# Layer 2's recurrence in a decoder kernel: exponentials of ramps on ScalarE, products on VectorE, squares on ScalarE

## The chip, the cores and the metric

The kernel runs on one core of a Trainium2 chip. TensorE (PE in the rows) multiplies matrices, VectorE (DVE), ScalarE (ACT) and GpSimd (POOL) work elementwise, and each has its own queue; semaphores order them. The metric is the device time of one launch in microseconds (us), the median of three runs.

## What is computed

The program is a whole four-layer decoder on 8 sequences of 256 tokens with 128 channels. The change is in one stage of it, layer 2's time mixing and channel mixing:

```python
def step(carry, kv):                      # over the 256 tokens
    aa, bb, pp = carry
    kk, vv = kv
    ww = u + kk
    p = jnp.maximum(pp, ww)
    e1 = jnp.exp(pp - p)
    e2 = jnp.exp(ww - p)
    out = (e1 * aa + e2 * vv) / (e1 + e2 + EPS_WKV)
    p2 = jnp.maximum(pp, kk)
    e1b = jnp.exp(pp - p2)
    e2b = jnp.exp(kk - p2)
    aa_new = e1b * aa + e2b * vv
    pp_new = p2 + jnp.log(e1b + e2b + EPS_WKV)
    return ((aa_new, bb_new, pp_new), out)
...
x = x + r * wkv_out                       # r a sigmoid
h2 = layer_norm(x, ln2_g, ln2_b)
kc = time_shift(h2, cmix_k) @ Wk_c.T      # 128 -> 512
rc = jax.nn.sigmoid(time_shift(h2, cmix_r) @ Wr_c.T)
vv = jnp.square(jax.nn.relu(kc)) @ Wv_c.T
x = x + rc * vv
```

## The kernel before

`time_mixing` is written by hand: each engine's instructions stand in the order of its own function (`pe`, `dve`, `act`, `pool`), and nothing reorders them. An engine that waits holds up all that stands behind it in its queue.

Channels lie on the 128 partitions. The 2048 tokens are four parts of 512 columns, two sequences each; `FIRST` is parts 0 and 1, `LAST` is 2 and 3. A part has seven tiles of 512 columns (`kk`, `v`, `r`, `d`, `c`, `m`, `num`) in scratch and three padded ones in w_early: `pm` (running maximum), `sp` (running sum), `aa` (running weighted sum). The recurrence over tokens is a scan along the columns, two per part (one for each sequence), so four kinds of scan: maximum, sum, sum again with the small constant added, weighted sum.

Between the scans stand weights. With pp the level before a token, the weights are exp(pp - max(pp, k)) and exp(k - max(pp, k)), and a third pair with k + u. Before the change VectorE forms the maximum and one difference, GpSimd the other difference (`decay_pool`), ScalarE the two exponentials in place (`weights_act`), GpSimd the products (`value_pool`, `num_pool`), VectorE the sum, a reciprocal and the last two products (`gate_dve`). The logarithm of the sum is ScalarE's (`logs_act`).

Then TensorE turns `num` back (`num_pe`), VectorE adds it to XN and takes the statistics (`residual_dve`, `variance_dve`), ScalarE takes the square root, both scale, TensorE turns the halves (`turn_half_pe`), VectorE applies gain and bias (`affine_dve`). "second" is this normalisation for FIRST, "later" for LAST. The channel mixing runs in four quarters of 512 tokens: `up_pe` makes four groups of 512 columns (two banks in turn) and the receptance product, ScalarE's relu empties them into KC, GpSimd squares them, `down_pe` multiplies by the second matrix, VectorE multiplies by the receptance and adds to X. TensorE's order is up(0), down(0), num(2), up(1), num(3), down(1), turn of the later half, then up and down of quarters 2 and 3.

In the rows, an operation of a helper has the helper's line: L2501 is every scan, L469 every matmul, L318 the scaling on VectorE.

## Time and profile before

| | |
|---|---|
| time, median of 3 (lowest to highest) | 2234.5 us (2232.88 to 2235.41) |
| profiled execution: its time, its span | 2244.19 us, 2242.4 us |
| mean granted TensorE clock, as a share of full speed | 0.911 |
| stage: first scan to last down product | 1194.9 to 1336.5 us of the span |

The times of rows are those of the profiled execution. A stage in the middle of the program moves the end by as much as it gets shorter, since the next one waits for its last result.

### The profile page before, as it was taken

Reading aid. Unit: us, or ns where it says so; the run is one execution under the profiler, and the core shown is the slowest. Engines: PE = TensorE matmul, PEld = TensorE weight load, DVE = VectorE, ACT = ScalarE, POOL = GpSimd, SP = SyncE. Lnnn points to the kernel's source line nnn. Section 1 sums busy time; section 2 is a strip of 40 time slices with the busy share of each in tenths; the row PEclk is TensorE's granted clock in tenths of the full one; section 3 lists DMA queues with packets and bytes.
Section 4 is the critical chain, followed back from the end, with each engine's and each line's share of the span. In section 5 each row is a group of like instructions: output and inputs, shape, how many; then the busy total and the mean of one; then the engine's idle time right before and its main releaser. Section 6 shows DMA issues by size and latency. Waiting matters only on the chain.

```text
span 2242.4 us, 37692 instructions
## 1 busy us (share of the span) xinstructions
PE 1885.0 (84%) x13296; PEld 1250.2 (56%) x13296; DVE 1558.1 (69%) x3633; ACT 1285.2 (57%) x2737; POOL 652.3 (29%) x616
## 2 busy tenths in 40 slices
PE   7999775988999999949974288999997997589886
PEld 5777562446777777524452165566665676434465
DVE  5777685866777677458758947989997456478543
ACT  5777533776888878617755236677665212247622
POOL 3223003203544434342004532444343001221043
PEclk9999896998999999969987599999999898779898
DMA  4000004411000000035101000000000100354102
GB/s 196 1 1 2 1 1 129 138 37 38 1 1 1 1 1 1 1 90 155 58 1 77 0 1 1 1 2 1 1 1 22 36 1 1 120 164 114 57 24 78
DMA packets 80153, 87.37 MB, mean 39 GB/s; under 512 B 6578, under 2 KB 70115, under 8 KB 79073
## 3 DMA queue, kind: packets, MB, share of 16 engines
q1 hardware_dynamic: 78625, 82.49, 11.7%
q0 software_dynamic: 1344, 2.49, 0.4%
...
## 4 chain that ended last, share of the span: by engine, by line
PE 53%; DVE 29%; ACT 7%; issue 6%; POOL 2%; DMA 2%; SPq 0%; another core or an unknown queue 0%; DVEq 0%; ACTq 0%; POOLq 0%
PE bank L469 45%; DVE scratch L1221 5%; PE bank L653 2%; ACT XN L1996 2%; PE bank L2934 2%; PE bank L368 2%; DVE scratch L3052 1%; DVE scratch L3072 1%; PE bank L693 1%; DVE stats L245 1%; DVE XN L3092 1%; DVE scratch L1608 1%; DVE w_keep L1895 1%; ACT L2074 1%; DVE w_early L2501 1%
## 5 line engine op out<-in xcount | busy, mean ns | idle before, releaser
L469 PE MATMUL bank<-scratch 64*128 64x256 bf16 (+7 forms) x3056 | 340.2, 306 | 67.5 <-DMA scratch<-parts 39.4
L1221 DVE TENSOR_REDUCE scratch<-bank 128x2 f32<-128x512 f32 x384 | 244.6, 686 | 82.4 <-PE bank L469 79.8
L469 PEld LDWEIGHTS bank<-scratch 64*128 64x128 bf16 (+4 forms) x3056 | 184.1, 122 | 195.7 <-DVE scratch L1221 73.9
L469 PE MATMUL bank<-w_keep,scratch 128*128 128x128 f32 (+4 forms) x1760 | 245.4, 330 | 18.4 <-DVE scratch L1938 4.1
L1307 ACT ACTIVATE w_keep<-bank 128x512 f32<-128x512 f32 x384 | 212.6, 597 | 52.0 <-PE bank L469 44.3
L469 PE MATMUL bank<-XNT,w_keep 128*128 128x256 f32 (+4 forms) x800 | 238.0, 437 | 4.5 <-POOL w_keep L2135 2.2
L469 PEld LDWEIGHTS bank<-w_keep,scratch 128*128 128x128 f32 (+3 forms) x1760 | 182.7, 184 | 84.0 <-issue 55.6
L469 PEld LDWEIGHTS bank<-XNT,w_keep 128*128 128x128 f32 x800 | 149.9, 197 | 57.7 <-issue 28.4
L469 PE MATMUL bank<-w_early,scratch 64*128 64x256 f32 (+3 forms) x1152 | 164.8, 346 | 20.4 <-ACT w_early L3152 8.7
L469 PEld LDWEIGHTS bank<-w_early,scratch 64*128 64x128 f32 (+3 forms) x1152 | 120.0, 185 | 66.4 <-issue 25.6
L469 PE MATMUL bank<-w_keep 128*32 128x256 f32 (+1 forms) x1600 | 124.3, 386 | 11.3 <-ACT w_keep L1307 5.4
L469 PE MATMUL bank<-scratch,w_early 128*128 128x256 f32 (+2 forms) x416 | 124.7, 444 | 10.5 <-DVE scratch L2496 3.8
L795 ACT ACTIVATE scratch<-bank,scratch 128x256 f32<-128x256 f32 x256 | 100.3, 474 | 54.8 <-DVE scratch L721 54.8
L721 DVE TENSOR_REDUCE scratch<-bank 128x2 f32<-128x512 f32 x128 | 82.5, 686 | 61.8 <-PE bank L469 61.6
L3152 ACT ACTIVATE w_early<-bank,scratch 128x256 f32<-128x256 f32 x172 | 82.9, 562 | 72.1 <-DVE scratch L3056 72.1
L469 PE MATMUL bank<-XNT,w_early 128*128 128x256 f32 (+1 forms) x384 | 118.4, 439 | 4.5 <-ACT XNT L383 1.6
L3261 POOL TENSOR_TENSOR w_early<-w_early,scratch 128x1024 f32<-128x1024 f32 x43 | 81.4, 1893 | 137.2 <-DVE scratch L3077 137.2
L368 PE MATMUL bank<-w_keep,XN 128*128 128x128 f32 x192 | 48.8, 430 | 80.0 <-DVE XN L318 77.1
L3052 DVE TENSOR_REDUCE scratch<-bank 128x2 f32<-128x512 f32 x128 | 87.6, 684 | 22.9 <-PE bank L469 22.9
L469 PEld LDWEIGHTS bank<-scratch,w_early 128*128 128x128 f32 x416 | 72.5, 200 | 51.1 <-issue 30.6
L735 POOL TENSOR_TENSOR scratch<-scratch 128x1024 f32<-128x1024 f32 x32 | 61.5, 1952 | 127.3 <-DVE scratch L751 127.3
L469 PEld LDWEIGHTS bank<-XNT,w_early 128*128 128x128 f32 x384 | 73.1, 201 | 44.7 <-issue 30.5
...
## 6 DMA issues: line engine op xcount, KB each, us to landing
...
```

The lines of the kernel that those rows point to most:

```text
L368: t = pe.transpose(k.bank[q][:, j * P:(j + 1) * P], src(i), k.w["ident"])
L469: return pe.matmul(out, lhsT, rhs, start=start, stop=stop, skip_group_check=True)
L653: m = pe.transpose(self.k.bank[3 + o][:, c * S + t * P:c * S + (t + 1) * P], self.expo[g % 4][:, t * S + c * P:t * S + (c + 1) * P], self. ...
L721: dve.tensor_reduce(self.neg[g % 4], self.scores(g)[:, :].rearrange("p (t s) -> p t s", s=S), AXX, ALU.max, negate=True).then_inc(*s.maxed ...
L735: return pool.tensor_tensor(self.kron[n][t].rearrange("p (h i j) -> p h i j", i=HD, j=HD), a, c, ALU.mult)
L795: a = act.activation(self.expo[g % 4][:, t * S:(t + 1) * S], self.scores(g)[:, t * S:(t + 1) * S], ACT.Exp, bias=self.neg[g % 4][:, t:t + 1])
L1221: dve.tensor_reduce(neg[:, :, h], self.k.bank[5 - g % 2][:, :].rearrange("p (t s) -> p t s", s=S), AXX, ALU.max, negate=True).then_inc(*s. ...
L1307: act.activation(self.expo[g % 8], k.bank[g % 4][:, :], ACT.Exp, scale=HD ** -0.5).then_inc(*s.weighed.up("e", g))
L1996: a = act.activation(self.by_head(self.early[u % 2])[:, t, h, :], self.upto, ACT.Copy, scale=a3[:, t, h:h + 1])
L3052: dve.tensor_reduce(neg, self.k.bank[o][:, :].rearrange("p (t s) -> p t s", s=S), AXX, ALU.max, negate=True).then_inc(*s.maxed.up("x", p, o))
L3152: a = act.activation(self.weights(p, o)[:, t * S:(t + 1) * S], self.k.bank[o][:, t * S:(t + 1) * S], ACT.Exp, bias=self.bias[p % 2][:, o * ...
L3261: pool.tensor_tensor(ex, ex, self.sums[p % 2].unsqueeze(2).to_broadcast([P, 2 * HALVES, S]), ALU.mult).then_inc(*s.pool.up("scaled", p))
```

## The change

The weights are written without a maximum. With x = k - pp, exp(pp - max(pp, k)) is exp(-relu(x)) and exp(k - max(pp, k)) is exp(-relu(-x)); the third pair has k + u in the place of k, which is a bias of u and of -u. So VectorE makes one difference x per part (`ahead_dve`), and ScalarE two relus and two exponentials for each pair (`ramps_act`). The level is not written back: the logarithm of the sum before the token is subtracted from x (`level_dve`). All products go from GpSimd to VectorE. The reciprocal becomes Ln and Exp with scale -1 on ScalarE (`inverse_act`); the square root and reciprocal of "second" and "later" become Ln and Exp with scale -0.5 (`log_root_act`). One table set with Ln and Exp is loaded ahead of the inputs and again after the sigmoids of `r`. The squares of the channel mixing go from GpSimd to ScalarE, each behind the next group's relu (`relu_act`, `square_act`), and the receptance sigmoids of quarters 0 and 1 behind all relus of the two. GpSimd keeps the folding of weights, with one more column (`minus_u`), and the four residual adds, each now as soon as the part's XN is there. The queues of VectorE, ScalarE and TensorE are written anew:

```diff
-    def first_decay_dve(dve, part):
-        (_, _, _, d, _, _, _), (pm, _, _) = streams[part]
+    def ahead_dve(dve, part):
+        (kk, v, r, d, c, x, num), (pm, sp, aa) = streams[part]
+        k3 = b3(kk)
+        dve.wait_ge(*s.stacked.at("in", part, 0))
+        scan(dve, part, pm, k3, k3, BEFORE_ALL, ALU.max, ALU.max).then_inc(*s.vector.up("p", part))
         dve.wait_ge(*s.vector.at("p", part))
-        dve.tensor_tensor(b3(d), pm[:, :, 0:S], pm[:, :, 1:PADDED], ALU.subtract).then_inc(*s.formed.up("d", part))
+        dve.tensor_tensor(b3(x), k3, pm[:, :, 0:S], ALU.subtract).then_inc(*s.formed.up("x", part))
...
+        dve.wait_ge(*s.vector.at("s", part))
+        dve.tensor_tensor(b3(num), b3(d), sp[:, :, 0:S], ALU.mult).then_inc(*s.vector.up("ds", part))
...
+    def level_dve(dve, part):
+        (kk, v, r, d, c, x, num), _ = streams[part]
+        dve.wait_ge(*s.scalar.at("log", part))
+        dve.tensor_tensor(x, x, num, ALU.subtract).then_inc(*s.formed.up("x2", part))
+
+    def weigh_dve(dve, part):
+        (kk, v, r, d, c, x, num), (pm, sp, aa) = streams[part]
+        dve.wait_ge(*s.weighed.at("second", part))
+        dve.wait_ge(*s.stacked.at("in", part, 1))
+        dve.tensor_tensor(c, c, v, ALU.mult).then_inc(*s.vector.up("cv", part))
+        dve.wait_ge(*s.vector.at("cv", part))
+        scan(dve, part, aa, b3(d), b3(c), 0.0, ALU.mult, ALU.add).then_inc(*s.vector.up("a", part))
+
+    def whole_dve(dve, part):
+        (kk, v, r, d, c, x, num), _ = streams[part]
+        dve.wait_ge(*s.weighed.at("third", part))
+        dve.scalar_tensor_tensor(out=x, in0=num, scalar=1e-8, in1=kk, op0=ALU.add, op1=ALU.add).then_inc(*s.vector.up("den", part))
+
+    def gate_dve(dve, part):
+        (kk, v, r, d, c, x, num), (pm, sp, aa) = streams[part]
+        dve.wait_ge(*s.vector.at("a", part))
+        dve.wait_ge(*s.vector.at("den", part))
+        dve.tensor_tensor(b3(num), b3(num), aa[:, :, 0:S], ALU.mult).then_inc(*s.vector.up("da", part))
+        dve.tensor_tensor(v, v, kk, ALU.mult).then_inc(*s.vector.up("vc", part))
+        dve.wait_ge(*s.vector.at("vc", part))
+        dve.wait_ge(*s.vector.at("da", part))
+        dve.tensor_tensor(num, num, v, ALU.add).then_inc(*s.vector.up("num", part))
+        dve.wait_ge(*s.scalar.at("inverse", part))
+        dve.wait_ge(*s.vector.at("num", part))
+        dve.tensor_tensor(num, num, x, ALU.mult).then_inc(*s.vector.up("out", part))
...
-        inverse_dve(k, dve, tag)
+        dve.wait_ge(*s.deviation.at(tag))
...
-        pe.wait_ge(*s.pool.at("squared", 4 * q + 3))
+        pe.wait_ge(*s.scalar.at("squared", 4 * q + 3))
...
+            ahead_dve(e, part)
+        for part in FIRST:
             sums_dve(e, part)
-        raised_dve(e, FIRST)
-        level_dve(e, FIRST)
-        raised_dve(e, LAST)
-        weigh_dve(e, FIRST)
-        level_dve(e, LAST)
-        gate_dve(e, FIRST)
-        weigh_dve(e, LAST)
+            raised_dve(e, part)
+        level_dve(e, 0)
+        sums_dve(e, 2)
+        level_dve(e, 1)
+        raised_dve(e, 2)
+        weigh_dve(e, 0)
+        sums_dve(e, 3)
+        whole_dve(e, 0)
+        weigh_dve(e, 1)
+        whole_dve(e, 1)
+        raised_dve(e, 3)
+        gate_dve(e, 0)
+        gate_dve(e, 1)
+        for part in LAST:
+            level_dve(e, part)
         residual_dve(e, "second", FIRST)
         scale_dve(k, e, "second", k.XN, O2, range(0, NT // 2))
+        weigh_dve(e, 2)
         affine_dve(e, "second", "r_g2", "r_b2", FIRST)
-        gate_dve(e, LAST)
+        weigh_dve(e, 3)
+        for part in LAST:
+            whole_dve(e, part)
+        for part in LAST:
+            gate_dve(e, part)
         residual_dve(e, "later", LAST)
...
+    def ramps_act(act, tag, part, x, down, up, first_bias, second_bias):
+
+        act.activation(down, x, ACT.Relu, bias=first_bias).then_inc(*s.lowered.up(tag, "down", part))
+        act.activation(up, x, ACT.Relu, bias=second_bias, scale=-1.0).then_inc(*s.lowered.up(tag, "up", part))
+        act.wait_ge(*s.lowered.at(tag, "down", part))
+        act.activation(down, down, ACT.Exp, scale=-1.0)
+        act.wait_ge(*s.lowered.at(tag, "up", part))
+        act.activation(up, up, ACT.Exp, scale=-1.0).then_inc(*s.weighed.up(tag, part))
+
+    def weights_act(act, tag, part):
+        (kk, v, r, d, c, x, num), _ = streams[part]
+        act.wait_ge(*s.formed.at("x" if tag == "first" else "x2", part))
+        if tag == "second":
+            act.wait_ge(*s.vector.at("s2", part))
+        if tag == "third":
+            ramps_act(act, tag, part, x, num, kk, w["r_u"], minus_u)
+        else:
+            ramps_act(act, tag, part, x, d, c, 0.0, 0.0)
+
+    def inverse_act(act, part):
+        (_, _, _, _, _, x, _), _ = streams[part]
+        act.wait_ge(*s.vector.at("den", part))
+        act.activation(x, x, ACT.Ln).then_inc(*s.lowered.up("den", part))
+        act.wait_ge(*s.lowered.at("den", part))
+        act.activation(x, x, ACT.Exp, scale=-1.0).then_inc(*s.scalar.up("inverse", part))
+
+    def log_act(act, part):
+        (_, _, _, _, _, _, num), (_, sp, _) = streams[part]
+        act.wait_ge(*s.vector.at("s2", part))
+        act.activation(b3(num), sp[:, :, 0:S], ACT.Ln).then_inc(*s.scalar.up("log", part))
+
+    def log_root_act(act, tag):
+        act.wait_ge(*s.variance.at(tag))
+        act.activation(k.rs[:, :], k.moments[:, 2, :], ACT.Ln, bias=k.small[:, 0:1], scale=1.0 / P).then_inc(*s.lowered.up("root", tag))
+        act.wait_ge(*s.lowered.at("root", tag))
+        act.activation(k.rs[:, :], k.rs[:, :], ACT.Exp, scale=-0.5).then_inc(*s.deviation.up(tag))
...
+        weights_act(e, "first", 0)
+        input_act(e, 3, 0)
+        weights_act(e, "first", 1)
+        input_act(e, 0, 1)
+        weights_act(e, "first", 2)
+        input_act(e, 1, 1)
+        weights_act(e, "first", 3)
+        input_act(e, 2, 1)
+        input_act(e, 3, 1)
...
+        log_act(e, 0)
+        log_act(e, 1)
+        weights_act(e, "second", 0)
+        weights_act(e, "second", 1)
+        weights_act(e, "third", 0)
+        weights_act(e, "third", 1)
+        log_act(e, 2)
+        inverse_act(e, 0)
+        inverse_act(e, 1)
...
+        e.preload_act_table_set("natural_log_exp_and_others")
+        log_act(e, 3)
+        weights_act(e, "second", 2)
+        weights_act(e, "second", 3)
+        log_root_act(e, "second")
+        scale_act(k, e, "second", k.XN, O2, range(0, NT // 2))
+        weights_act(e, "third", 2)
+        weights_act(e, "third", 3)
+        relu_act(e, 0)
+        relu_act(e, 1)
+        inverse_act(e, 2)
+        relu_act(e, 2)
+        inverse_act(e, 3)
+        for u in (3, 4, 5):
+            relu_act(e, u)
+        log_root_act(e, "later")
+        scale_act(k, e, "later", k.XN, O2, range(NT // 2, NT))
+        for u in (6, 7):
+            relu_act(e, u)
+        for q in range(QUARTERS):
+            if q >= 2:
+                for u in range(4 * q, 4 * q + 4):
+                    relu_act(e, u)
+            receptance_act(e, q)
...
+    def relu_act(act, u):
+        q, g = divmod(u, 4)
+        act.wait_ge(*s.projected.at("kc", u))
+        if q >= 2 and g == 0:
+            act.wait_ge(*s.multiplied.at("vv", q - 2))
+        act.activation(KC[q % 2][:, g * BANK:(g + 1) * BANK], k.bank[u % 2][:, :], ACT.Relu).then_inc(*s.gated.up("relu", u))
+        if g:
+            square_act(act, u - 1)
+        if g == 3:
+            square_act(act, u)
+
+    def square_act(act, u):
+        q, g = divmod(u, 4)
+        kg = KC[q % 2][:, g * BANK:(g + 1) * BANK]
+        act.wait_ge(*s.gated.at("relu", u))
+        act.activation(kg, kg, ACT.Square).then_inc(*s.scalar.up("squared", u))
...
-            for g in range(4):
-                u, kg = 4 * q + g, KC[q % 2][:, g * BANK:(g + 1) * BANK]
-                e.wait_ge(*s.gated.at("relu", u))
-                e.tensor_tensor(kg, kg, kg, ALU.mult).then_inc(*s.pool.up("squared", u))
+            e.wait_ge(*s.added.at("num", q))
```

VectorE, where parts 0 and 1 are divided and gated. Before (L2549 sum, L2551 reciprocal, L2554 and L2557 products, L2501 the weighted scan of part 2):

```order
L2549 SCALAR_TENSOR_TENSOR scratch<-scratch 128x512
L2551 RECIPROCAL scratch<-scratch 128x512
L2554 TENSOR_TENSOR scratch<-scratch 128x512
L2557 TENSOR_TENSOR scratch<-scratch 128x512
L2549 SCALAR_TENSOR_TENSOR scratch<-scratch 128x512
L2551 RECIPROCAL scratch<-scratch 128x512
L2554 TENSOR_TENSOR scratch<-scratch 128x512
L2557 TENSOR_TENSOR scratch<-scratch 128x512
L2501 SCALAR_TENSOR_TENSOR w_early<-scratch 128x256 x2
```

and now (L2552 and L2553 the two products, L2556 their sum, L2559 times the inverse, L2562 times `r`, L2533 the level of parts 2 and 3):

```order
L2552 TENSOR_TENSOR scratch<-scratch,w_early 128x512
L2553 TENSOR_TENSOR scratch<-scratch 128x512
L2556 TENSOR_TENSOR scratch<-scratch 128x512
L2559 TENSOR_TENSOR scratch<-scratch 128x512
L2562 TENSOR_TENSOR scratch<-scratch 128x512
L2552 TENSOR_TENSOR scratch<-scratch,w_early 128x512
L2553 TENSOR_TENSOR scratch<-scratch 128x512
L2556 TENSOR_TENSOR scratch<-scratch 128x512
L2559 TENSOR_TENSOR scratch<-scratch 128x512
L2562 TENSOR_TENSOR scratch<-scratch 128x512
L2533 TENSOR_TENSOR scratch<-scratch 128x512 x2
```

The reciprocals have gone from VectorE's queue, GpSimd's three products and sums of each part have come into it, and the weighted scans of parts 2 and 3 stand further back.

ScalarE, where the logarithms and the second weights of parts 0 and 1 stand. Before (L2741 Ln, L2748 and L2749 exponentials, L2751 the added u):

```order
L2741 ACT_TABLE_LOAD
L2741 ACTIVATE scratch<-w_early 128x512 x2
L2748 ACT_TABLE_LOAD
L2748 ACTIVATE scratch<-scratch 128x512
L2749 ACTIVATE scratch<-scratch 128x512
L2751 ACTIVATE scratch<-scratch,w_keep 128x512
L2748 ACTIVATE scratch<-scratch 128x512
L2749 ACTIVATE scratch<-scratch 128x512
L2751 ACTIVATE scratch<-scratch,w_keep 128x512
L2741 ACT_TABLE_LOAD
```

and now (L2710 copies of v, L2741 Ln, L2714 and L2715 relus, L2717 and L2719 exponentials):

```order
L2710 ACTIVATE scratch<-bank 128x512 x2
L2741 ACTIVATE scratch<-w_early 128x512 x2
L2714 ACTIVATE scratch<-scratch 128x512
L2715 ACTIVATE scratch<-scratch 128x512
L2717 ACTIVATE scratch<-scratch 128x512
L2719 ACTIVATE scratch<-scratch 128x512
L2714 ACTIVATE scratch<-scratch 128x512
L2715 ACTIVATE scratch<-scratch 128x512
L2717 ACTIVATE scratch<-scratch 128x512
```

Three table loads have gone here, and each pair of exponentials has two relus ahead of it.

ScalarE, at the first quarter of the channel mixing. Before (L2759 relu, L2763 sigmoid):

```order
L284 ACTIVATE small<-small 128x1
L2759 ACTIVATE scratch<-bank 128x512 x4
L2763 ACTIVATE scratch<-bank 128x512
L2759 ACTIVATE scratch<-bank 128x512 x4
L2763 ACTIVATE scratch<-bank 128x512
```

and now (L2809 relu, L2819 square, L2734 Ln and L2736 Exp of the inverse of parts 2 and 3):

```order
L2809 ACTIVATE scratch<-bank 128x512 x2
L2819 ACTIVATE scratch<-scratch 128x512
L2734 ACTIVATE scratch<-scratch 128x512
L2736 ACTIVATE scratch<-scratch 128x512
L2809 ACTIVATE scratch<-bank 128x512
L2819 ACTIVATE scratch<-scratch 128x512
L2734 ACTIVATE scratch<-scratch 128x512
L2736 ACTIVATE scratch<-scratch 128x512
L2809 ACTIVATE scratch<-bank 128x512
L2819 ACTIVATE scratch<-scratch 128x512 x2
```

The squares and two inverses now stand between the relus; the sigmoids have moved behind quarter 1.

TensorE, from the end of down(0) to the end of down(1), as a difference (L2613 and L2618 are `num_pe`, L2620 and L2625 `turn_half_pe`; the 512-wide matmuls are up(1), the x16 row is down(1)):

```order
-L2613 MATMUL bank<-w_keep,scratch 128x128 x4
+L2618 MATMUL bank<-w_keep,scratch 128x128 x8
 L469 MATMUL bank<-scratch,w_early 128x512 x8
 L469 MATMUL bank<-w_early,scratch 128x128 x8
-L2613 MATMUL bank<-w_keep,scratch 128x128 x4
+L2625 MATMUL bank<-w_keep,scratch 128x128 x8
 L469 MATMUL bank<-w_keep,scratch 128x128 x16
-L2620 MATMUL bank<-w_keep,scratch 128x128 x8
```

num(3) has moved ahead of up(1), and the later half's transposes ahead of down(1).

## Rows read from the trace of the kernel before

**Rows 1.** The page, busy time, share and instructions by engine.

```profile
PE 1885.0 (84%) x13296; PEld 1250.2 (56%) x13296; DVE 1558.1 (69%) x3633; ACT 1285.2 (57%) x2737; POOL 652.3 (29%) x616
```

**Rows 2.** Windows: length, PE PEld DVE ACT POOL busy (count), clock, DMA, GB/s.

```profile
1194.00:1208.50 14.50, 14.50 (x33) 6.33 (x32) 11.49 (x14) 7.50 (x13) 5.90 (x5) 0.92 0.00 1
1208.50:1268.80 60.30, 7.95 (x22) 3.68 (x20) 59.21 (x58) 24.08 (x37) 32.89 (x22) 0.57 0.00 0
1268.80:1280.40 11.60, 2.06 (x8) 1.50 (x8) 10.70 (x26) 5.69 (x10) 8.40 (x7) 0.50 0.00 0
1280.40:1286.00 5.60, 5.54 (x8) 2.48 (x9) 5.43 (x5) 0.60 (x1) 1.05 (x1) 0.58 0.00 0
1286.00:1337.00 51.00, 49.43 (x266) 34.14 (x264) 22.48 (x48) 17.37 (x29) 21.02 (x20) 1.00 0.00 1
```

**Rows 3.** Groups by line, VectorE, 1208.5 to 1268.8: busy, mean ns, idle before.

```profile
L2501 DVE TENSOR_TENSOR_SCAN w_early<-scratch 128x256 f32<-128x256 f32 x22 | 19.4, 933 | 0.4 <-ACT scratch L2705 0.2
L2551 DVE RECIPROCAL scratch<-scratch 128x512 f32<-128x512 f32 x2 | 6.7, 3353 | 0.1
```

**Rows 4.** One line of VectorE: min/median/max ns, first and last start.

```profile
L2531 DVE TENSOR_TENSOR scratch<-w_early,scratch x4: 692/1079/1632, 1221.6 to 1246.6; 128x512 f32<-128x512 f32 x4
```

**Rows 5.** Timeline of VectorE: start us, us, line, operation, idle before.

```profile
1207.04 1.28 DVE L2501 TENSOR_TENSOR_SCAN w_early<-scratch 128x256 f32<-128x256 f32 x2 [0.39 <-ACT scratch L2705]
...
1218.32 0.67 DVE L2518 TENSOR_TENSOR scratch<-scratch 128x512 f32<-128x512 f32 x1
1219.01 0.69 DVE L2520 SCALAR_TENSOR_TENSOR scratch<-scratch 128x512 f32<-128x512 f32 x1
1219.74 1.27 DVE L2501 TENSOR_TENSOR_SCAN w_early<-scratch 128x256 f32<-128x256 f32 x2
1220.93 0.67 DVE L2529 TENSOR_TENSOR w_early<-w_early,scratch 128x512 f32<-128x512 f32 x1
...
1222.97 1.67 DVE L2529 TENSOR_TENSOR w_early<-w_early,scratch 128x512 f32<-128x512 f32 x1
...
1268.83 0.68 DVE L2566 TENSOR_TENSOR XN<-XN,bank 128x512 f32<-128x512 f32 x1
...
1272.37 1.24 DVE L256 TENSOR_TENSOR moments<-moments 128x16 f32<-128x16 f32 x1
...
1276.09 2.38 DVE L318 TENSOR_SCALAR scratch<-XN,rs,moments 128x128 f32<-128x128 f32 x5
1278.74 1.66 DVE L2496 TENSOR_SCALAR scratch<-bank,w_keep 128x512 f32<-128x512 f32 x2 [0.27 <-PE bank L2620]
```

**Rows 6.** Timeline of GpSimd.

```profile
1222.40 1.68 POOL L2771 TENSOR_TENSOR scratch<-w_early,scratch 128x512 f32<-128x512 f32 x1 [5.86 <-DVE scratch L2531]
```

**Rows 7.** Timeline of ScalarE.

```profile
1198.80 0.60 ACT L2698 ACTIVATE scratch<-bank 128x512 f32<-128x512 f32 x1 [1.12 <-PE bank L469]
...
1204.57 1.28 ACT L2704 ACT_TABLE_LOAD   x1
1205.86 0.63 ACT L2704 ACTIVATE scratch<-scratch 128x512 f32<-128x512 f32 x1
1206.40 0.61 ACT L2705 ACTIVATE scratch<-scratch 128x512 f32<-128x512 f32 x1
...
1225.48 0.71 ACT L2751 ACTIVATE scratch<-scratch,w_keep 128x512 f32<-128x512 f32 x1
...
1274.87 0.31 ACT L278 ACTIVATE rs<-moments,small 128x16 f32<-128x16 f32 x1 [2.22 <-DVE moments L258]
```

**Rows 8.** One line of ScalarE, Square of 128x512 in another stage.

```profile
L2031 ACT ACTIVATE w_keep<-scratch x32: 612/613/663, 555.2 to 930.6; 128x512 f32<-128x512 f32 x32
```

**Rows 9.** Timeline of TensorE: up(0), up(2), down(3).

```profile
1280.46 9.42 PE L469 MATMUL bank<-scratch,w_early 128*128 128x512 f32 x16 [0.90 <-DVE scratch L2496]
...
1311.24 7.13 PE L469 MATMUL bank<-scratch,w_early 128*128 128x512 f32 x16 [1.00 <-DVE scratch L2496]
...
1332.69 3.84 PE L469 MATMUL bank<-w_keep,scratch 128*128 128x128 f32 x32
```

156 lines of the change are left out of this document (20 added, 136 removed).

## The prediction

> **What bounds the kernel now.** I began with the busy shares [rows 1]: TensorE has most of the span, so a change that touches VectorE, ScalarE and GpSimd can only pay where TensorE waits for them. The table of windows over this stage shows where that is [rows 2]. From 1208.5 to 1268.8 TensorE is busy 7.95 of 60.3 us and VectorE 59.21: the recurrence runs at VectorE's pace. From 1286 to 1337 it is the reverse (TensorE 49.43 of 51.0 us). So two places count: the instant at which the channel mixing starts on TensorE, now 1280.46 [rows 9], and the length of its tail, which ends at 1332.69 + 3.84 = 1336.5 [rows 9], 56.1 us later.
>
> Next I asked why VectorE needs 60 us. The window has 58 instructions [rows 2]. A pair of scans alone takes 1.27 us and a two-input instruction of 512 columns 0.67 [rows 5]; 22 scans, two reciprocals (6.7 us [rows 3]) and 34 others make 14.0 + 6.7 + 22.8 = 43.5 us. VectorE was busy 59.2, so 15.7 us are excess; the scans alone show 19.4 for 14.0 [rows 3], and line 2531 lies between 692 and 1632 ns for one shape [rows 4]. The pattern is in the timeline: line 2529 at 1220.93 takes 0.67; the same line at 1222.97 takes 1.67 [rows 5], and a GpSimd tensor_tensor ran from 1222.40 to 1224.08 [rows 6]. 1224.08 plus 0.58 is 1224.66, when the slow one ended. VectorE stood still until GpSimd was done.
>
> **A rule beside it.** The Trainium skill, SBUF — State Buffer, section "SBUF: two separate sides", says the same as a rule: the port pair is an exclusive lock for a whole instruction, between GpSimd and a VectorE instruction with two SBUF inputs. By that rule the excess goes with GpSimd's work; were it instead the cost of these access patterns, the sum would be that of the second rival below.
>
> **The change, step by step.** Steps between instructions, from the four consecutive rows 1218.32 to 1220.93 [rows 5]: 0.70 us where the next waits for the result (0.73 for scalar_tensor_tensor), 1.19 for a scan pair, so 0.60 for each instruction whose successor doesn't wait. On ScalarE an activation of 512 columns starts 0.54 after the one before [rows 7]; I use 0.52, the step when the later one needs 0.61, and allow 0.15 more for a Ln whose Exp waits.
>
> *A, the head.* Before, the first weights wait for a table load at 1204.57 [rows 7] and the sums start at 1207.04 [rows 5]. After, the table is loaded in ScalarE's idle time before the first copy. The third copy is at 1198.80 [rows 7]; the four activations of part 0 follow (2.1 us, to 1201.4), then the copy of part 3, to 1202.0. VectorE then does that part's two scans and its subtraction (1.27 + 0.04 + 0.58) and starts the sums at 1203.9. Part 0's weights were ready 2 us earlier. Gain 3.2 us.
>
> *B, VectorE's queue from the sums to the first residual.* Before it is 1207.04 to 1268.83 [rows 5], 61.8 us. After, by the order, it has 50 instructions: 7 for each of four parts (sums and raised), 4 subtractions (level), 3 for each of parts 0 and 1 (weigh), 2 (whole), 10 (gate). 22 have a successor that waits, 4 of them scalar_tensor_tensor: 18 x 0.70 + 4 x 0.73 + 28 x 0.60 = 32.3 us. No GpSimd instruction runs here, so no excess. Gain 29.5 us. Check by what goes away: 15.7 excess, 6.9 of reciprocals (two, 3.35 and a gap each), and 58 other instructions become 50, which is the remaining 7. The divisions go to ScalarE as Ln and Exp. Does it keep pace? Per part and tag a ramp costs 4 x 0.52 = 2.1 us. Following both queues, part 0's second weights are ready at 1215.9 and wanted at 1218.9, part 1's third at 1222.4 and wanted at 1225, and the receptance copies, with a 1.28 us load [rows 7] on either side, end about 1230 and are wanted at 1231. ScalarE has 2 to 3 us in hand, 1 us at the last; so its 12 ramps (25 us) and the two loads cost nothing. Without that cover each us would count.
>
> *C, normalisation.* Before, 11.6 us [rows 2]. The two small instructions held up at 1272.37 (1.24 us and the next like it) [rows 5], against 0.17 free, give back 2.1; the scale, 2.38 with GpSimd at work [rows 5], gives back 1.0 (estimate: five steps of 0.27). Square root and reciprocal become Ln and Exp of 128x16: 0.31 by the nearest row [rows 7], about 0.1 more than before. The weigh of part 2 now stands between scale and affine: 0.70 + 1.19 = 1.9, of which 0.5 covers the wait for the transposes that the affine had at 1278.74 [rows 5]. GpSimd's residual add of part 1 now runs while the variance starts: +0.3. Sum 10.2, gain 1.4. New waits here are ScalarE's: behind its wait for the variance stand the third ramps of parts 2 and 3 and the first relu; ScalarE is free 3.4 us ahead of the mixing's start, the relu's input comes 3.8 us after it, and the two ramps need 4.2 of those 7.2 us.
>
> *D, the tail.* TensorE's matmuls are the same. One wait goes: the 1.00 us before 1311.24 [rows 9], since the later half's transposes now stand ahead of the second down product, which covers VectorE's affine. One comes: down(0) waits for the last square. On ScalarE, after relu 1 come squares, relus and two Ln-Exp pairs, ten more activations, about 12.1 us after the start; TensorE arrives at 11.2. Cost 0.95. In later quarters only two squares follow the last relu: 0.60 + 2 x 0.52 + 0.1 = 1.75 us against the 1.8 us of receptance matmuls, like GpSimd's square now. A Square from SBUF is 613 ns at another line [rows 8]. The transposes num(2) and num(3) find VectorE finished 3 us earlier. Relus 6 and 7 stand behind ScalarE's wait for the later variance: root and scale end 26 us after the start, as relu 7's input comes. The receptance sigmoids of quarters 0 and 1 now stand behind those relus and a table load; what they hold up, two products of VectorE, isn't wanted by TensorE until quarter 2's receptance matmuls, 10 us later. Net 0.
>
> Sum 3.2 + 29.5 + 1.4 + 0 = 34.1 us. The profiled execution took 2244.2 us (span 2242.4), 9.7 above the median of 2234.5; a sum of rows from it should read 2210 there and 2200.4 as a median.
>
> **Bounds.** ScalarE's ramps may cost 0.71 a step, the price of its one activation with a per-partition bias, without overlap [rows 7]: then the first ramps, the root, and the ten activations before down(0) all lengthen, 3.8 us in all: 2204.2. TensorE's clock is 0.50 before the mixing, 0.58 until 1286 and 1.00 after [rows 2]. If it rises at once at the start, the first 5.3 us of matmuls shrink by half (−2.6); if 3 us later, +1.5. If down(0) doesn't wait, −0.95. So 2197 to 2205.5 as the likeliest case's own range.
>
> **Rivals.**
> *ScalarE becomes the bound* (8%): 40 us of activations stand in 51 us. At 0.6 us a step it still hides; at 1.0 each wait for weights opens and the gain falls to 15: 2219. For it: three times as many exponentials and relus. Against: the rows of 0.61 to 0.63.
> *The excess isn't GpSimd's* (4%): if shape or address makes 15.7 us, they stay: 2216. Against: the same line at 0.67 and 1.67.
> *The clock doesn't come up* (2%), the one that ends slower. Place: the mixing's start, after idle time with only eight transposes in it. Tail matmuls busy 49.4 us at 1.00 [rows 2] would need up to 49 us more at 0.50: 2234.5 − 34 + 49 = 2249. It decides from 34 us of work at the low clock. Against: the same sequence of transposes, scale, transposes, affine rose within 5.5 us now. The Trainium skill, TensorE: Matmul & The Clock Gate, section "What's actually happening", states that throttled is the default and activity releases it; this trace agrees, 0.50 then 1.00.
> *More goes than I count* (8%): the clock comes early and part 3's work is better hidden: 2195 to 2197.
> The likeliest has 78%. About 0.2% (4.5 us) is what a measurement can tell here: faster 96%, same 2%, slower 2%. Range 2195.5 to 2205.5.
>
> **What would show it.** Right: between the sums and the first residual VectorE has no instruction of 512 columns over 0.75 us, and about 32 us pass; the mixing starts near 1246; ScalarE never ends a VectorE wait over 1 us before that; one gap of about 1 us ahead of down(0), none ahead of up(2). Wrong: activations steps over 0.6 us, long scans with GpSimd idle, a table load between relus, or a PEclk under 1.00 more than 8 us into the mixing.

## The result, and the profile after

The changed kernel takes 2193.26 us, the median of 4 runs (2191.42 to 2196.38), against 2234.78 us for the kernel before (4 runs): a ratio of 0.9817, 95% interval 0.98 to 0.9834. The sign and the mechanism were as forecast; the gain, 41.5 us, is larger than the 34.1 us of the sum, and the time lies below the range. The profiled execution took 2194.88 us where 2210 was forecast for it.

The windows over the stage, cut where its phases change, answer to [rows 2]:

```profile
1195.30:1208.50 13.20, 13.20 (x32) 5.85 (x31) 12.13 (x19) 10.30 (x21) 0.00 (x0) 0.98 0.01 2
1208.50:1236.50 28.00, 7.86 (x22) 3.71 (x20) 27.24 (x44) 20.25 (x35) 0.00 (x0) 0.64 0.00 0
1236.50:1246.20 9.70, 2.17 (x9) 1.49 (x8) 8.87 (x28) 9.13 (x20) 2.54 (x2) 0.50 0.00 0
1246.20:1249.70 3.50, 3.50 (x4) 1.51 (x5) 3.46 (x6) 1.04 (x3) 0.00 (x0) 0.50 0.00 0
1249.70:1300.80 51.10, 50.22 (x269) 34.88 (x267) 19.75 (x51) 26.40 (x48) 2.54 (x2) 0.99 0.00 1
```

VectorE is still what sets the pace up to the mixing (27.24 of 28.0 us busy), but the stretch is less than half as long (28.0 us for 60.3). GpSimd is silent in it. The mixing is TensorE's, as before.

VectorE's timeline answers to [rows 5]: the start of the sums, the first residual, the variance, scale and affine, and the only wait over 1 us before the gating of part 3 is done (1259.2).

```profile
1203.92 1.27 DVE L2503 TENSOR_TENSOR_SCAN w_early<-scratch 128x256 f32<-128x256 f32 x2
...
1236.57 0.68 DVE L2571 TENSOR_TENSOR XN<-XN,bank 128x512 f32<-128x512 f32 x1
...
1239.68 0.44 DVE L252 TENSOR_TENSOR moments<-stats 128x16 f32<-128x16 f32 x1
...
1241.45 1.37 DVE L318 TENSOR_SCALAR scratch<-XN,rs,moments 128x128 f32<-128x128 f32 x5
...
1244.64 1.50 DVE L2498 TENSOR_SCALAR scratch<-bank,w_keep 128x512 f32<-128x512 f32 x2
...
1254.38 0.69 DVE L2559 TENSOR_TENSOR scratch<-scratch 128x512 f32<-128x512 f32 x1 [3.21 <-ACT scratch L2736]
```

From 1203.92 to 1236.57 are 32.65 us, forecast 32.3. The one long wait, 3.21 us for L2736 (the inverse of part 2), begins after the mixing has started, and TensorE wants that part only at 1261.79.

The groups of VectorE in that stretch answer to [rows 3] and [rows 4]; the columns are busy us, mean ns:

```profile
L2503 DVE TENSOR_TENSOR_SCAN w_early<-scratch 128x256 f32<-128x256 f32 x20 | 12.5, 675 | 0.2
L2533 DVE TENSOR_TENSOR scratch<-scratch 128x512 f32<-128x512 f32 x4 | 2.6, 680 | 0.0
```

ScalarE's timeline answers to [rows 7]: first weights, a ramp with a per-partition bias, the two table loads around the receptance copies, and the square root's place.

```profile
1188.52 1.28 ACT L2756 ACT_TABLE_LOAD   x1
...
1199.31 0.62 ACT L2714 ACTIVATE scratch<-scratch 128x512 f32<-128x512 f32 x1
1199.83 0.62 ACT L2715 ACTIVATE scratch<-scratch 128x512 f32<-128x512 f32 x1
...
1218.55 0.70 ACT L2714 ACTIVATE scratch<-scratch,w_keep 128x512 f32<-128x512 f32 x1
...
1226.62 0.63 ACT L2736 ACTIVATE scratch<-scratch 128x512 f32<-128x512 f32 x1
1227.27 1.28 ACT L2710 ACT_TABLE_LOAD   x1
1228.57 2.06 ACT L2710 ACTIVATE scratch<-bank 128x512 f32<-128x512 f32 x4
1230.65 1.28 ACT L2779 ACT_TABLE_LOAD   x1
...
1240.65 0.31 ACT L2745 ACTIVATE rs<-moments,small 128x16 f32<-128x16 f32 x1 [0.30 <-DVE moments L258]
```

A step is 0.52 us (1199.31 to 1199.83), or 0.61 with the bias of u (1218.55 to 1219.16). TensorE's timeline answers to [rows 9]:

```profile
1246.20 9.25 PE L469 MATMUL bank<-scratch,w_early 128*128 128x512 f32 x16 [2.30 <-DVE scratch L2498]
...
1258.11 3.84 PE L469 MATMUL bank<-w_keep,scratch 128*128 128x128 f32 x32 [0.87 <-ACT scratch L2819]
...
1271.32 1.04 PE L2625 MATMUL bank<-w_keep,scratch 128*128 128x128 f32 x8
1272.19 3.74 PE L469 MATMUL bank<-w_keep,scratch 128*128 128x128 f32 x32
1275.76 7.03 PE L469 MATMUL bank<-scratch,w_early 128*128 128x512 f32 x16
...
1296.95 3.28 PE L469 MATMUL bank<-w_keep,scratch 128*128 128x128 f32 x27
```

The mixing starts at 1246.20 (forecast: near 1246), there is one gap, 0.87 us ahead of down(0), and none ahead of up(2) at 1275.76.

**The ledger of the stage.** Measured in each trace from GpSimd's first instruction of the stage (1180.94 before, 1180.49 after), so that what lies ahead of it drops out:

| phase | before | after | gain | forecast |
|---|---|---|---|---|
| A, to the first sum | 26.10 | 23.43 | 2.67 | 3.2 |
| B, to the first residual | 61.79 | 32.65 | 29.14 | 29.5 |
| C, to the mixing | 11.63 | 9.63 | 2.00 | 1.4 |
| D, to the end of down(3) | 56.07 | 54.59 | 1.48 | 0 |
| stage | 155.59 | 120.30 | 35.29 | 34.1 |

The spans of the two profiled executions differ by 49.3 us (2242.4 and 2193.1). 0.45 lie ahead of the stage, 35.3 in it, and 13.6 behind it, where no instruction was changed. Two places hold nearly all of the 13.6. The first is the next stage. Its first TensorE work, of before:

```profile
1344.20 1.96 PE L368 MATMUL bank<-w_keep,XN 128*128 128x128 f32 x8 [7.67 <-DVE XN L318]
...
1349.60 3.75 PE L469 MATMUL bank<-w_keep,scratch 128*128 128x512 f32 x4 [1.19 <-DVE scratch L3046]
```

and after:

```profile
1308.07 1.96 PE L368 MATMUL bank<-w_keep,XN 128*128 128x128 f32 x8 [7.28 <-DVE XN L318]
...
1313.47 1.95 PE L469 MATMUL bank<-w_keep,scratch 128*128 128x512 f32 x4 [1.30 <-DVE scratch L3065]
```

The four matmuls at 1349.60 took 3.75 us, the same ones at 1313.47 take 1.95. That is 1.8 of a 2.2 us difference; the other 0.4 lie in the idle time ahead of the first transposes (7.67 and 7.28). The second is the program's last stage. A window that ends 35 us before the end, of before and then after:

```profile
2177.40:2207.40 30.00, 24.62 (x119) 18.22 (x120) 7.71 (x24) 9.65 (x19) 14.85 (x16) 0.77 0.11 30
```

```profile
2128.10:2158.10 30.00, 28.38 (x172) 22.52 (x173) 9.08 (x27) 12.65 (x24) 22.90 (x23) 1.00 0.17 48
```

Before had 119 matmuls there at a clock of 0.77, after has 172 at 1.00. TensorE's rows around the start of that window, of before:

```profile
2175.85 0.33 PE L3665 MATMUL bank<-w_keep 128*128 128x128 f32 x1
...
2177.79 1.16 PE L469 MATMUL bank<-w_keep,w_early 128*128 128x320 f32 x3 [1.15 <-issue]
2179.95 1.46 PE L469 MATMUL bank<-w_keep,w_early 128*128 128x320 f32 x2 [1.00 <-issue]
...
2193.13 0.49 PE L3665 MATMUL bank<-w_keep 128*128 128x128 f32 x3
```

and of the second profile of the same kernel (the first run of the next section):

```profile
2175.73 0.44 PE L3665 MATMUL bank<-w_keep 128*128 128x128 f32 x2
...
2181.16 0.49 PE L3665 MATMUL bank<-w_keep 128*128 128x128 f32 x3
```

The same work takes 17.3 us in the first profile of before and 5.4 in its second (5.4 in the changed kernel too): a loss of 11.9 us. Behind this place the changed kernel takes 0.7 more, so 11.2 of the 13.6 lie in the last stage.

### The profile page after: what moved, and what is told of

It is laid out like the page before. It is cut to its first block, busy times and chain, and to the rows that moved or that the text cites. A ratio compares the mean times of both kernels' runs of the same rounds, so it can differ in the third digit from the quotient of the medians.

```text
span 2193.1 us, 37675 instructions
## 1 busy us (share of the span) xinstructions
PE 1875.5 (86%) x13296; PEld 1246.2 (57%) x13296; DVE 1522.1 (69%) x3631; ACT 1299.4 (59%) x2773; POOL 588.4 (27%) x569
## 4 chain that ended last, share of the span: by engine, by line
PE 54%; DVE 28%; ACT 7%; issue 5%; POOL 3%; DMA 2%; SPq 0%; DVEq 0%; POOLq 0%; ACTq 0%
PE bank L469 45%; DVE scratch L1221 5%; PE bank L653 2%; ACT XN L1996 2%; DVE scratch L3071 2%; PE bank L368 2%; DVE scratch L3091 2%; PE bank L2953 2%; PE bank L693 1%; DVE stats L245 1%; DVE XN L3111 1%; DVE scratch L1608 1%; DVE w_keep L1895 1%; ACT L2074 1%; PE bank L1190 1%
## 5 line engine op out<-in xcount | busy, mean ns | idle before, releaser
L469 PE MATMUL bank<-w_keep 128*32 128x256 f32 (+1 forms) x1600 | 124.2, 386 | 11.2 <-ACT w_keep L1307 5.4
L1895 DVE SCALAR_TENSOR_TENSOR w_keep<-w_keep,w_early 128x256 f32<-128x256 f32 x192 | 97.2, 556 | 0.1
```

Of the source, the lines that this page charges most:

```text
L469: return pe.matmul(out, lhsT, rhs, start=start, stop=stop, skip_group_check=True)
L1895: o = dve.scalar_tensor_tensor(out=yv[:, j, :], in0=xv[:, j, tap:tap + S], scalar=scale, in1=yv[:, j, :], op0=ALU.mult, op1=ALU.add)
```

## The experiments

Each kernel was compared with runs of the kernel before on the same chip; three chips were used, on which the kernel before read 2231.9 us (17 runs; the two repeats, products, squares), 2229.83 us (7 runs; reciprocal, order, inverses, folding) and 2244.08 us (9 runs; the last four). So a time is read through its ratio, and through the length of the stage in its trace. The changed kernel as it is ran on the first of the three only, so the edited ones of the other two are set against it by ratio and by stage.

### The two kernels again

The kernel before, unchanged.

> The kernel before, unchanged, for a second profile. The change gained 41.5 us, of which its own stage shows 35.3 and 6 us lie in later stages that it doesn't touch. Theory (the surplus is not the change's: TensorE's clock and one stall in the last stage fell unluckily in the profile shown): the ratio is 1.00 within 0.2%, this profile's stage again takes 155.6 us from its first instruction to the last down product, and the 11 us that the first profile lost between 2178 and 2204 us are mostly gone. Rival (the change does something for the later stages): the loss of 11 us between 2178 and 2204 is there again.

Measured: 2233.76 us (10 runs), ratio 1.0011, interval 0.9997 to 1.0025; stage 155.69 us. Its profiled execution has a span of 2230.6 where the first one had 2242.4, and the same window of the last stage reads

```profile
2165.60:2195.60 30.00, 28.22 (x170) 22.11 (x169) 9.25 (x27) 13.13 (x25) 23.00 (x24) 1.00 0.17 48
```

with 170 matmuls at 1.00. The loss of 11.9 us is not the kernel's. Nor is it one execution's alone: on the third chip the kernel before reads 2244, and the four profiles taken there (the last four runs) all show such a loss, with 119 to 125 matmuls at a clock of 0.77 to 0.83 in this window.

The changed kernel, unchanged.

> The changed kernel, unchanged, for a second profile. Theory: ratio 0.981 to 0.985; the stage takes 120.3 us again within 0.3; what differs from the first profile differs in the later stages, where the low stretches of TensorE's clock lie elsewhere. Rival: all of it repeats to 0.5 us, later stages too, so that the 6 us are a fixed property of the program.

Measured: 2193.93 us (2189.6 to 2196.8), ratio 0.984, interval 0.9812 to 0.9868; stage 120.17 us. On this chip the gain in medians is 2231.9 - 2193.9 = 38.0 us. The two repeated profiles differ by 35.5 us in the stage and by 2.5 behind it (894.1 and 891.6 us from the last down product to the end), and the four matmuls of the next stage again take 3.75 and 1.95. So what lies behind the stage repeated nearly as the rival had it (892.3 and 891.6 in the two profiles of the changed kernel), but only 2.5 of the expectation's 6 us are there.

### Who held VectorE up

The kernel before, with the products and differences of the recurrence moved from GpSimd to VectorE; reciprocals, maxima and exponentials stay. For each part:

```diff
+        dve.wait_ge(*s.vector.at("s", part))
+        dve.tensor_tensor(b3(m), b3(d), sp[:, :, 0:S], ALU.mult).then_inc(*s.vector.up("ds", part))
...
+            dve.tensor_tensor(b3(d), P0, b3(m), ALU.subtract)
...
+            dve.tensor_tensor(c, c, v, ALU.mult).then_inc(*s.vector.up("cv", part))
...
+            dve.tensor_tensor(b3(num), b3(d), aa[:, :, 0:S], ALU.mult).then_inc(*s.vector.up("da", part))
+            dve.tensor_tensor(v, v, c, ALU.mult).then_inc(*s.vector.up("vc", part))
+            dve.tensor_tensor(num, num, v, ALU.add).then_inc(*s.vector.up("num", part))
...
-        decay_pool(e, "second", FIRST)
-        value_pool(e, FIRST)
-        decay_pool(e, "third", FIRST)
-        num_pool(e, FIRST)
...
```

> The kernel before with only GpSimd's elementwise work of the recurrence moved to VectorE, in its place in the order (maxima, differences, reciprocals and GpSimd's squares stay). Theory (VectorE stood still for GpSimd): between the sums and the first residual VectorE gets 22 instructions more (+14.3 us) and loses the excess of 15.7 us, no 512-column instruction except the reciprocals over 0.75 us; the normalisation loses 3 us more: 4 to 6 us faster, ratio 0.997 to 0.998. Rival (the long instructions are long by shape or address): they stay long, 14 us slower, ratio 1.006.

Measured: 2222.67 us, ratio 0.9962, interval 0.9944 to 0.9979; stage 148.97 us, 6.6 shorter (3.0 between the sums and the first residual, 3.6 in the normalisation), somewhat more than the 4 to 6 expected. VectorE's groups from the sums to the first residual, and the window:

```profile
L2501 DVE TENSOR_TENSOR_SCAN w_early<-scratch 128x256 f32<-128x256 f32 x24 | 15.3, 678 | 2.0 <-ACT scratch L2716 1.7
L2564 DVE RECIPROCAL scratch<-scratch 128x512 f32<-128x512 f32 x2 | 6.7, 3352 | 0.1
L2533 DVE TENSOR_TENSOR scratch<-w_early,scratch 128x512 f32<-128x512 f32 x4 | 2.8, 692 | 0.1
L2531 DVE TENSOR_TENSOR w_early<-w_early,scratch 128x512 f32<-128x512 f32 x4 | 2.7, 680 | 0.0
1207.00:1266.30 59.30, 9.95 (x26) 4.48 (x25) 57.53 (x83) 26.19 (x40) 0.00 (x0) 0.59 0.00 0
```

L2531 and L2533 here are the lines 2529 and 2531 of before. The second of them took 692 to 1632 ns for one shape [rows 4] and takes 692 on average now; scans have gone from 933 [rows 3] to 678. From the first sum (1207.54 here) to the first residual (1266.29) VectorE has 82 instructions where it had 60, and needs 58.75 us where it needed 61.79. The 22 added ones cost about 14 us (estimate: 0.60 to 0.70 each), so about 17 of excess went with GpSimd's work, for the 15.7 of the sum. The excess was GpSimd's; that shapes or addresses make it is refuted. The Trainium skill, SBUF — State Buffer, section "SBUF: two separate sides", describes this as a lock that whoever starts first holds for the whole instruction. The traces agree: L2529 took 1.67 us at 1222.97 beside a GpSimd instruction of 1.68 [rows 5] [rows 6], and takes 0.68 on average here, with GpSimd silent.

The same numbers give the worth of the rest, by subtraction and not by a run of its own: from this kernel's 58.75 us to the changed kernel's 32.65 are 26.1 us, of which the reciprocals are 6.4 (next run) and about 20 are the 30 instructions that the ramps and the new differences make needless.

### The divisions on VectorE

The changed kernel, with the reciprocals back on VectorE and the inverses gone from ScalarE.

```diff
-        dve.wait_ge(*s.scalar.at("inverse", part))
-        dve.wait_ge(*s.vector.at("num", part))
+        dve.reciprocal(x, x).then_inc(*s.vector.up("inverse", part))
+        dve.wait_ge(*s.vector.at("inverse", part))
```

> The changed kernel with the divisions back as reciprocals on VectorE (3.35 us each), no Ln and Exp for them. Theory (the sum's term of 6.9 us for two reciprocals is right, those of parts 2 and 3 lie beside TensorE's up(0) and down(0)): the first residual comes 6.9 us later; in the tail the gap ahead of down(0) goes (-0.9) and num(3) may come up to 1.2 us late; stage 127 us against 120.3. Rival (the Ln and Exp pairs only moved the time to ScalarE): stage below 123.

Measured: 2202.15 us, ratio 0.9882, interval 0.9853 to 0.9911; stage 127.16 us, 6.9 longer: 6.4 before the first residual, 0.4 in the tail, where the gap ahead of down(0) is gone and one of 0.89 us stands ahead of num(3). ScalarE is freer by two pairs of activations before that residual and gives nothing for it. So the inverses on ScalarE are hidden, and the part of B that the prediction put to the reciprocals, 6.9, measures 6.4.

### The squares on GpSimd

The changed kernel, with the squares where they were: `square_act` isn't called, GpSimd waits for each relu and multiplies, `down_pe` waits for GpSimd. GpSimd's residual adds stand behind the squares again.

```diff
-        if g:
-            square_act(act, u - 1)
-        if g == 3:
-            square_act(act, u)
...
+            for g in range(4):
+                u, kg = 4 * q + g, KC[q % 2][:, g * BANK:(g + 1) * BANK]
+                e.wait_ge(*s.gated.at("relu", u))
+                e.tensor_tensor(kg, kg, kg, ALU.mult).then_inc(*s.pool.up("squared", u))
```

> The changed kernel with the squares of the channel mixing back on GpSimd. Theory: the gap ahead of down(0) shrinks from 0.9 us to near 0, since a GpSimd square ends 1.7 us after the last relu's input and TensorE has 1.8 us of receptance matmuls; VectorE's gating of parts 2 and 3 gets 1 us instructions here and there under cover. Against the changed kernel 0 to 1 us faster: ratio 0.981 to 0.983. Rival (the squares on ScalarE bring part of the gain): ratio over 0.985.

Measured: 2198.8 us (2192.44 to 2199.34), ratio 0.9853, interval 0.9825 to 0.9881; stage 119.97 us, 0.3 shorter. down(0):

```profile
1247.39 9.44 PE L469 MATMUL bank<-scratch,w_early 128*128 128x512 f32 x16 [2.30 <-DVE scratch L2498]
1256.67 1.95 PE L469 MATMUL bank<-w_early,scratch 128*128 128x128 f32 x16
1258.97 3.28 PE L469 MATMUL bank<-w_keep,scratch 128*128 128x128 f32 x27 [0.35 <-POOL scratch L2838]
```

It waits 0.35 us instead of 0.87. In the stage, moving the squares brought nothing and costs 0.3 us, but that isn't all down(0)'s: 0.26 of it lie in the normalisation, where the residual add no longer stands in the way of L252 (0.19 us here, 0.44 in the changed kernel), and in quarters 2 and 3 the squares on ScalarE save 0.16. The ratio came out on the rival's side (over 0.985), and the median 4.9 us above the changed kernel's on the same chip; the intervals overlap, and the profiles differ by 2.8 us ahead of the stage and 3.8 behind it, where the two programs are the same. So the runs can't tell the two kernels apart.

### TensorE's order of before

The changed kernel, with num(3) behind up(1) and the later half's transposes behind down(1) again; ScalarE's relus 6 and 7 stand ahead of its later scale, as they must then.

```diff
         num_pe(e, 2)
+        up_pe(e, 1)
         num_pe(e, 3)
-        up_pe(e, 1)
+        down_pe(e, 1)
         turn_half_pe(e, "later", (2, 3))
-        down_pe(e, 1)
...
```

> The changed kernel with TensorE's order of before: num(3) behind up(1), the later half's transposes behind down(1), and ScalarE's relus 6 and 7 ahead of its wait for the later variance. Theory (the tail's 1.5 us come from the order: a wait of 1.0 us ahead of up(2) gone, and transposes that take 0.87 us of TensorE where I had counted 1.57): the wait of 1.0 us is back, the tail from up(0) to the last down product is 56 us against 54.6, the stage 121.7 us. Rival (the order does nothing, the tail got shorter elsewhere): 54.6 again.

Measured: 2199.75 us, ratio 0.9858, interval 0.9826 to 0.9891; stage 122.58 us, 2.3 longer, nearly all of it in the tail (56.8 against 54.6; expected 121.7 and 56). The transposes of the later half and up(2):

```profile
1278.43 1.57 PE L2625 MATMUL bank<-w_keep,scratch 128*128 128x128 f32 x8 [0.26 <-DVE scratch L318]
1281.01 7.14 PE L469 MATMUL bank<-scratch,w_early 128*128 128x512 f32 x16 [1.00 <-DVE scratch L2498]
```

The order is worth the 1.00 us ahead of up(2) and, beside it, 0.26 of waiting and 0.70 of the transposes themselves: from 1278.43 to the wait ahead of 1281.01 they hold TensorE 1.58 us, where in the changed kernel down(1) starts 0.87 after them. That is 2.0 of the 2.2.

### The inverses ahead of the relus

The changed kernel, with the divisions of parts 2 and 3 ahead of the first relu instead of between relus.

```diff
+        inverse_act(e, 2)
+        inverse_act(e, 3)
         relu_act(e, 0)
         relu_act(e, 1)
-        inverse_act(e, 2)
         relu_act(e, 2)
-        inverse_act(e, 3)
```

> The changed kernel with ScalarE's inverses of parts 2 and 3 ahead of relu 0, where ScalarE is idle, and not between the relus of quarter 0. Theory: down(0) waits only because ten activations stand behind relu 1; with six the gap of 0.87 us ahead of it goes, and VectorE's wait of 3.2 us for the inverse of part 2 too: stage 119.4 us. Rival (relu 0, now later, holds up TensorE's third group): a new gap inside up(0) and 120.3 or more.

Measured: 2199.36 us, ratio 0.9855, interval 0.9821 to 0.9889; stage 119.45 us. The gap ahead of down(0) is gone, as expected, and the stage 0.85 us shorter; yet the time isn't lower. In the profile, 3.7 us more pass behind the stage than in the changed kernel's: the matmuls that took 1.95 us there take 3.75, and those behind them are slow too.

### The column of minus u folded last

The changed kernel, with GpSimd's new instruction behind the folding of weights.

```diff
-        pool.tensor_scalar(minus_u, w["r_u"], -1.0, None, ALU.mult)
         for name, (mix, now, prev, less) in folded.items():
...
+        pool.tensor_scalar(minus_u, w["r_u"], -1.0, None, ALU.mult).then_inc(*s.preset.up("minus_u"))
...
+            act.wait_ge(*s.preset.at("minus_u"))
```

> The changed kernel with GpSimd's new instruction for -u last in the folding instead of first. In the changed kernel VectorE's ten scalings ahead of the affine take 4.14 us against 3.33 before, and the first matmul comes 0.95 us later after the stage's start. Theory (GpSimd's folding, moved by 0.16 us by the added instruction, now falls on these scalings): 3.3 us again, first matmul 9.5 to 9.7 us after the stage's first instruction, stage 119.4 to 119.9. Rival (chance of the execution): 4.1 us again and 120.3.

Measured: 2195.02 us, ratio 0.9848, interval 0.9817 to 0.9879; stage 120.17 us. In the changed kernel VectorE's ten scalings of L351 take 4.14 us in sum where they took 3.33, and TensorE's first input matmul stands 10.45 us after the stage's start instead of 9.50. Here both are as before (3.33, 9.50), so the added instruction was the cause; but only 0.4 us of the 0.95 reach the first sum and 0.1 the stage's end, and the stage isn't the 119.4 to 119.9 that I expected. The granted clock shows why. From the first input matmul to the first scan, in this kernel:

```profile
1189.10:1193.52 4.42, 4.42 (x6) 1.84 (x7) 2.41 (x11) 0.60 (x1) 0.00 (x0) 0.50 0.49 211
1193.52:1196.42 2.90, 2.90 (x6) 1.22 (x5) 1.96 (x3) 0.60 (x1) 0.00 (x0) 0.72 0.00 0
```

and in the changed one:

```profile
1190.94:1195.36 4.42, 4.42 (x6) 1.84 (x7) 2.42 (x11) 0.60 (x1) 0.00 (x0) 0.50 0.24 104
1195.36:1197.73 2.37, 2.37 (x6) 1.08 (x5) 1.96 (x3) 0.60 (x1) 0.00 (x0) 0.89 0.00 0
```

The same twelve matmuls take 7.32 and 6.79 us: TensorE starts earlier and stays longer at the low level.

### The next stage's clock

Three kernels test whether the 1.95 us of the next stage's first matmuls hang on when that stage starts. The changed kernel, with two, four or eight products more on VectorE between the stage's last addition and its statistics; nothing uses them.

```diff
             e.wait_ge(*s.added.at("out", q))
+            if q == 3:
+                for n in range(2):
+                    e.tensor_tensor(RC[0], RC[1], RC[1], ALU.mult).then_inc(*s.vector.up("delay", n))
+                    e.wait_ge(*s.vector.at("delay", n))
             stats_dve(k, e, "next", k.X, range(4 * q, 4 * q + 4))
```

> The changed kernel, and on VectorE two products of 128x512 more (0.70 us each), after the last addition of the stage's channel mixing and before its statistics; they delay the next stage's start by 1.4 us and compute nothing that is used. Theory (the next stage's short low stretch of the clock, 6.8 us, is had only when its first transposes come soon enough after the drop): the drop stays 4.3 to 4.9 us after the last down product, the transposes stand 8.7 us after it, and the low stretch becomes 13.7 us, so the first four matmuls of 512 columns take 3.7 us where they took 1.95, and the time rises by 1.4 + 2.2 = 3.6 us or more against the changed kernel: about 2197. Rival (the shorter stretch comes from something else that the change did in the stage): 6.8 us stays, the time rises by 1.4 us alone, about 2195.

> As the one with two products, but four of them, a delay of 2.8 us. Theory: low stretch 13.7 us, ending about 18 us after the last down product; the first four matmuls of the next stage begin 15.5 us after it and are all at the low clock (3.75 us), about 2.8 + 1.8 = 4.6 us over the changed kernel: about 2198. Rival: 2.8 us alone, 2196.

> As the one with two products, but eight of them, a delay of 5.6 us. Theory: the first matmuls of 512 columns begin 18.3 us after the last down product, when a low stretch of 13.7 us that began 4.4 us after it has just ended (18.1), so they run at the full clock (1.95 us) again and only the delay is paid: 5.6 us over the changed kernel, 2199. If the stretch lasts yet longer (about 20 us) because no transposes stood in it, they take 3.75 and it is 2201 or more. Rival (not a matter of the instant): 5.6 us alone, 1.95.

Measured: 2208.7 us, ratio 0.9842 (0.982 to 0.9863); 2214.47, ratio 0.9873 (0.9852 to 0.9894); 2210.22, ratio 0.9849 (0.9828 to 0.9871). The expectations' absolute times were for another chip. The first matmuls of the next stage with two products:

```profile
1312.44 1.96 PE L368 MATMUL bank<-w_keep,XN 128*128 128x128 f32 x8 [8.83 <-DVE XN L318]
...
1317.84 3.75 PE L469 MATMUL bank<-w_keep,scratch 128*128 128x512 f32 x4 [1.20 <-DVE scratch L3069]
```

and with eight:

```profile
1312.10 1.96 PE L368 MATMUL bank<-w_keep,XN 128*128 128x128 f32 x8 [13.09 <-DVE XN L318]
...
1317.50 3.35 PE L469 MATMUL bank<-w_keep,scratch 128*128 128x512 f32 x4 [1.20 <-DVE scratch L3069]
```

The stage itself is unchanged (120.4, 120.2, 120.1 us). Read in windows of 0.5 us, the granted clock falls 4.3 us after the last down product in all three, as in the changed kernel. It comes back 6.8 us later in the changed kernel, 13.7 with two products, 17.1 with four and with eight. Beside the other profiles (us after the last down product):

| clock falls | first transposes | clock low for | kernels |
|---|---|---|---|
| 4.3 to 4.9 | 7.2 to 7.4 | 6.8 | changed (both profiles), squares, reciprocals, folding |
| 4.3 | 8.8 | 13.7 | two products |
| 4.3 | 10.1 and 13.1 | 17.1 | four, eight products |
| 2.1 to 3.2 | 7.2 to 7.7 | 13.7 | before (both profiles), products on VectorE, order, both small edits |
| 5.3 | 7.5 | 13.7 | inverses |

With the fall at 4.3 to 4.9 us, the five profiles without a delay have the short stretch and the three with one a long one: the stage of the changed kernel is not enough to make it short. But the start of the next stage doesn't decide alone. Where the clock fell earlier or later the stretch was long without any delay, in six profiles. What sets the instant of the fall is not known. Nor is the chip excluded: the delayed kernels ran on the third chip only, and the changed one never did.

My expectations for four and eight products were wrong in their number: I had 13.7 for both, and for eight the full clock in the first four matmuls, where the chip gave 17.1 and 3.35 us. VectorE's reduction of a bank that starts at 1335.06 in the changed kernel stands later behind the stage's end by 3.4, 5.7 and 7.2 us. The first transposes stand 1.5, 2.8 and 5.8 later; the other 1.9, 2.9 and 1.4 are the price of the clock. Over all that follows the stage, the four and the eight products read the same (910.3 and 910.4 us). That the median with eight lies 4 us below that with four is more than these two traces show, and is not explained.

### Both small edits together

The changed kernel with the inverses ahead of the relus and the column of minus u last.

> The changed kernel with both small edits: the inverses of parts 2 and 3 ahead of the first relu, and the column of minus u folded last. Stage 119.4 us, 0.7 shorter than the changed kernel's. If the next stage's clock behaves as in the run with the inverses alone (drop about 5.5 us after the last down product, low 13.7 us), the time is 2197, no better than the changed kernel; if as in the run with the folding alone (low 6.8 us), 2192.5.

Measured: 2206.18 us (2197.51 to 2208.71), ratio 0.982, interval 0.9794 to 0.9845. The stage is the shortest of all, 119.25 us, 1.05 less than the changed kernel's, and the ratio is that of the changed kernel within its interval. Its next stage starts at the low clock too (3.50 us for the four matmuls), though the fall came 2.1 us after the last down product, at neither of the two instants that I had expected. No version here beats the changed kernel by an amount that the runs can tell.

## Why the prediction was right, and where it failed

**The step that failed** is the term for the rest of the program, which the prediction put at nothing: "a sum of rows from it should read 2210 there and 2200.4 as a median" takes the rest as rigid, so that the end moves by what the stage gains and by no more. What the runs showed in its place differs for the two figures.

For the 2210: the profile after has 13.6 us less behind the stage. 11.2 of them lie in the last stage, by a loss that the first profile of before happened to have and its second had not, and 2.2 at the start of the next stage (1.8 of clock, 0.4 of idle time). The loss is also of the size of the 9.7 us by which that profiled execution stood above the median: these were not a constant of both kernels.

For the 2200.4, which doesn't rest on the 9.7: the median is 2193.26, 7.1 lower. 1.2 of it are the stage's own (35.3 for 34.1), 2.2 are the next stage's start, which the second pair of profiles shows too, and 3.7 stand in no trace. On one chip, the gain in medians is 38.0 us, and the profiles there have 35.5 in the stage and 2.5 behind it. In the first comparison it is 41.5; the kernel before read 2.9 us higher there than on that chip, with the changed kernel within 0.7. Why single executions of the kernel before spread from 2224 to 2247 us over the chips stays open. So does what made the clock's low stretch short behind the changed stage; nothing in the prediction brought it about, and three edited kernels (order, inverses, both small edits) don't have it, so as far as the runs show these 1.8 us are luck.

**A, the head, 2.67 for 3.2.** The table load is out of the way, as said, and the sums follow the last input part. Not foreseen: the added column on GpSimd, in the way of VectorE's scalings, puts the first input matmul 0.95 us later; the input matmuls' clock gives more than half of it back, so 0.4 is what it costs at this point, by the run with the folding.

**B, VectorE's queue, 29.14 for 29.5.** Right in its mechanism and sum. The excess was GpSimd's (shown by the products alone; about 17 us for the 15.7), the reciprocals' part is 6.4 where I had 6.9 (shown by the reciprocals alone), and no instruction of 512 columns is over 0.69 us. What the fewer other instructions bring is read off by subtraction only. ScalarE kept pace, as worked out: 0.52 and 0.61 a step, no wait of VectorE for it over 1 us between the sums and the mixing. Its rival of 8% is refuted.

**C, the normalisation, 2.0 for 1.4.** The terms of the prediction sum to 1.3, not 1.4. As said: the small instructions are free (2.1), the scale takes 1.37 instead of 2.38. The rest lies in four places: L297 was held up too before (0.60 us to the next start, now 0.21), which the sum left out; from the affine's start to the mixing 0.16 less pass; GpSimd's add in the way of L252 (0.44 us) costs 0.13 where I had 0.3; and root and reciprocal cost no more than before where I had 0.1 more. Scale and weigh together gave 0.14 less than forecast.

**D, the tail, 1.48 for 0.** Two of its three signs were right: the gap ahead of up(2) is gone (1.00), and the one ahead of down(0) came (0.87, forecast 0.95). The term mis-sized was the later half's transposes: I let them cost the same in their new place, and they cost 0.7 less, with 0.2 less at the end of down(1) ahead of them. up(0) is 0.16 shorter, up(2) 0.10, and the receptance products of quarters 2 and 3 0.15 together, which is the squares' part. With the wait ahead of down(0) against them, these make the 1.48.

**The clock.** It came up 4.3 us into the mixing, 4.6 before the change (windows of 0.5 us), and stayed, so the 2% rival is out. The rival "more goes than I count", 2195 to 2197, had the right sign, but named the wrong place: the clock that came early was the next stage's.
